# VectorE sums weight and difference for the last twelve weight batches, attention weights loaded in 256 KB transfers, new hand-written orders

## What is computed

```python
x = x + _layernorm(_L0_attn_ref(_layernorm(x), W_qkv, W_out))
x = x + _layernorm(_L0_ffn_ref(_layernorm(x), w_gate_up, w_proj))
# attention: qkv = x @ W_qkv.T ; q, k = phi(q), phi(k)
#   out = q * cumsum(k*v) / (q * cumsum(k) + eps), then @ W_out.T
# feed-forward: weights pass through a per-group ternary quantization
w_g = w.astype(bfloat16).reshape(-1, 64)
scale = clip(mean(abs(w_g)), 1e-8)
w_hat = clip(round(w_g / scale), -1, 1) * scale
wq = w + stop_gradient(w_hat - w)          # all in bfloat16
h = silu(x @ gate) * (x @ up); out = rms_norm(h) @ wq_proj.T
```

## Time and profile before

| what | value |
|---|---|
| median of three runs | 1160.17 us |
| profiled execution, its own time | 1160.26 us |
| its span, first to last instruction | 1158.4 us |
| mean granted TensorE clock | 0.984 of full |
| TensorE matmul busy | 1098.9 us (95%), 5376 matmuls |
| VectorE busy | 772.9 us (67%) |
| ScalarE, GpSimd busy | 442.3 us, 534.2 us |

### The profile page before, as it was taken

One profiled execution on the slowest core, in us unless ns is written; L12 is line 12 of the kernel. 1 busy time (PEld: TensorE's weight loads), 2 busy tenths in 40 slices (PEclk: granted clock), 3 DMA queues, 4 the chain that ended last, 5 costly groups with the idle time before them and its releaser, 6 DMA issues. The chain is left out here.

```text
span 1158.4 us, 14626 instructions
## 1 busy us (share of the span) xinstructions
PE 1098.9 (95%) x5376; PEld 659.5 (57%) x5376; DVE 772.9 (67%) x1224; ACT 442.3 (38%) x752; POOL 534.2 (46%) x493
## 2 busy tenths in 40 slices
PE   6997779998999999999999999999999999899997
PEld 5886355554566864468544774458644684454443
DVE  5999988985668687438872588527863488435323
ACT  3443546665522133422443234431444134333432
POOL 2548789977344343415434254415334253224323
PEclk9998889999999999999999999999999999899999
DMA  7021234200030210002100210002100010100001
GB/s 253 29 73 37 79 88 143 74 29 1 1 109 1 73 37 1 1 1 73 37 1 1 74 37 1 1 1 73 37 1 1 16 58 1 37 1 1 37 1 37
DMA packets 29079, 44.98 MB, mean 39 GB/s; under 512 B 1360, under 2 KB 9552, under 8 KB 29008
## 3 DMA queue, kind: packets, MB, share of 16 engines
q1 hardware_dynamic: 29008, 44.05, 11.7%
HBM read 34.60 MB, written 9.44 MB: 38 GB/s over the span
## 5 line engine op out<-in xcount | busy, mean ns | idle before, releaser
L540 PE MATMUL bank<-x3t,wgu_t 128*128 128x512 f16 x1536 | 351.1, 382 | 11.2 <-ACT ht L946 9.0
L540 PEld LDWEIGHTS bank<-x3t,wgu_t 128*128 128x128 bf16 x1536 | 149.1, 99 | 194.8 <-ACT ht L946 13.9
L1235 POOL TENSOR_TENSOR acc<-acc,ht 128x512 f32<-128x512 f32 x90 | 114.6, 1274 | 270.5 <-ACT ht L987 270.3
L576 PE MATMUL bank<-wproj_t,hid 128*128 128x512 bf16 x872 | 204.8, 380 | 3.3 <-ACT wproj_t L866 3.3
L1594 DVE TENSOR_TENSOR ht<-ht,bank 128x512 f32<-128x512 f32 x112 | 76.1, 679 | 159.8 <-PE bank L540 127.3
L521 PE MATMUL bank<-xnt,wqkv_hi 128*128 128x512 f32 x672 | 168.1, 392 | 0.0
L576 PEld LDWEIGHTS bank<-wproj_t,hid 128*128 128x128 f16 x872 | 85.2, 98 | 104.3 <-issue 4.5
L521 PEld LDWEIGHTS bank<-xnt,wqkv_hi 128*128 128x128 f32 x672 | 125.1, 188 | 26.0 <-issue 0.4
L1600 DVE TENSOR_TENSOR hid<-ht,hid 128x512 f16<-128x512 f32 x109 | 90.6, 831 | 66.3 <-ACT hid L974 66.3
L974 ACT ACTIVATE hid<-ht 128x512 f16<-128x512 f32 x109 | 68.5, 629 | 160.7 <-DVE ht L1594 160.7
L1181 POOL TENSOR_TENSOR tk<-tq,ts 128x512 f32<-128x512 f32 x28 | 55.0, 1965 | 136.6 <-DVE ts L1509 112.7
(11 more groups left out here) (178 smaller groups left out, 1558.2 us busy)
## 6 DMA issues: line engine op xcount, KB each, us to landing
raw_q<-in_L_ffn_w_gate_up_dram SPq DMA_DIRECT2D x32, 256.0 KB, 2.8
xn<-in_L_attn_x_dram SPq DMA_DIRECT2D x7, 1024.0 KB, 5.1
out_dram<-xn SPq DMA_DIRECT2D x7, 1024.0 KB, 8.8
x<-in_L_attn_x_dram SPq DMA_DIRECT2D x6, 1024.0 KB, 6.6
raw_q<-in_L_ffn_w_proj_dram SPq DMA_DIRECT2D x16, 256.0 KB, 2.9
raw_a<-in_L_attn_W_qkv_dram SPq DMA_DIRECT2D x4, 768.0 KB, 8.1
xn<-in_L_attn_x_dram SPq DMA_DIRECT2D x4, 256.0 KB, 3.2
raw_out<-in_L_attn_W_out_dram SPq DMA_DIRECT2D x1, 1024.0 KB, 9.7
```

The source lines that it names most:

```text
L540: last = pe.matmul(bank[:], wgu_t[:, k, first_row:first_row + P], x[:, part, k], start=(n == 0), stop=(n == 2 * KD - 1))
L576: last = pe.matmul(bank[:], hid_of(f, part, k)[:, t * P:(t + 1) * P], wproj_t[:, k], start=(k == 0 and part == 0), stop=(k == MT - 1 and p ...
L1235: pool.tensor_tensor(acc[:], acc[:], ht_of(f)[:, m % 2], ALU.add).then_inc(q["acc_done"], 1)
```

## The change

- **Sum on VectorE.** For batches 12 to 23, a new VectorE call `whole(b)` follows `diff(b)`: yq plus wb into yq, in bfloat16, 128 x 1024. `transpose_half` then waits for `q_whole` and transposes yq alone: 4 matmuls for a half in place of 8. Batches 0 to 11 stay as they are.
- **Attention weights in 256 KB transfers.** Sixteen transfers with a semaphore each in place of five; nine ahead of the wait on the first transposes and seven behind it, as many bytes on each side as before. `transpose_raw(r)` waits for its own tile.
- **Two waits on ScalarE.** `hidden_square` of m == 0 waits for the hidden value alone (`h_done`) in every chunk, no longer for the low part; `hidden_gate` of m == 2 now waits for that low part in every chunk.
- **Orders.** The four lists of `start()` are set anew: the same calls, apart from the twelve `whole`.

```diff
-        raw_a_in = [sem(f"raw_a_in{i}") for i in range(KD + 1)]
+        raw_a_in = [sem(f"raw_a_in{r}") for r in range(4 * KD)]
+        SUMMED = 12
+        q_whole = sem("q_whole")
@@ SyncE
-            def load_raw(i):
-
-                if i < KD:
-                    rows = w_qkv.rearrange("(s j p) k -> p j s k", s=3, p=P)[:, i]
+            def load_raw(r):
+
+                if r < NG:
+                    j, part = divmod(r, 3)
+                    rows = w_qkv[part * D + j * P:part * D + (j + 1) * P, :]
                 else:
-                    rows = w_out.rearrange("(t p) k -> p t k", p=P)
-                sp.dma_start(raw_a[i][:], rows).then_inc(raw_a_in[i], 16)
+                    j, part = KD, r - NG
+                    rows = w_out[part * P:(part + 1) * P, :]
+                sp.dma_start(raw_a[j][:, part], rows).then_inc(raw_a_in[r], 16)
...
-            load_raw(0)
-            load_raw(1)
-            load_raw(2)
+            for r in range(0, 9):
+                load_raw(r)
             sp.wait_ge(t1_done, KD)
             sp.dma_start(xn[:], x_ch[1]).then_inc(x_loaded, 16)
-            load_raw(3)
-            load_raw(4)
+            for r in range(9, 16):
+                load_raw(r)
@@ TensorE
-                    if i == 0:
+                    if i == 0 and b < SUMMED:
                         pe.wait_ge(q_diff, b + 1)
+                    elif i == 0:
+                        pe.wait_ge(q_whole, b - SUMMED + 1)
...
-                        for part, w in enumerate(PLACES[b]):
-                            last = pe.matmul(ps[3][:, n * P:(n + 1) * P], w[:, cols], turned, start=(part == 0), stop=(part == 1))
+                        parts = PLACES[b] if b < SUMMED else PLACES[b][1:]
+                        for part, w in enumerate(parts):
+                            last = pe.matmul(ps[3][:, n * P:(n + 1) * P], w[:, cols], turned,
+                                             start=(part == 0), stop=(part == len(parts) - 1))
...
-                transpose_raw(0, 1), transpose_x_at(0, 0, 1, 2, 3), transpose_raw(2, 3, 4, 5), group_at(0, 0), transpose_raw(6, 7, 8)
+                transpose_raw(0, 1, 2), transpose_x_at(0, 0, 1, 2, 3), transpose_raw(3, 4, 5, 6), group_at(0, 0), transpose_raw(7)
...
-                group_at(1, 0, 1, 2, 3, 4, 5, 6), project_att_at(0, 0, 1, 2, 3), group_at(1, 7, 8, 9, 10), transpose_half(0, 0, 1)
+                transpose_raw(12, 13, 14, 15), group_at(0, 8), transpose_x_at(1, 0, 1, 2, 3), group_at(0, 9, 10, 11), group_at(1, 0, 1, 2, 3, 4)
+                project_att_at(0, 0, 1, 2, 3), group_at(1, 5, 6, 7, 8, 9, 10), transpose_half(0, 0, 1), transpose_x1_at(0, 0, 1, 2, 3)
...
-                transpose_half(22, 0), gate_unit(0, 15), transpose_half(22, 1), project_first(12), up_unit(0, 15), project_first(13)
+                gate_unit(1, 9), gate_unit(0, 15), transpose_half(22, 1), project_first(12, 13), up_unit(1, 9), up_unit(1, 10)
@@ ScalarE
                 elif m == 2:
                     act.wait_ge(q["sq_done"], at(MT, c, 0))
-                    if f < 2:
-                        act.wait_ge(q["h_lo"], 1)
+                    act.wait_ge(q["h_lo"], at(MT, c, 0))
...
-                if f < 2 and m == 0:
-                    act.wait_ge(q["h_done"], 1)
+                if m == 0:
+                    act.wait_ge(q["h_done"], at(MT, c, 0))
                 else:
                     act.wait_ge(q["h_lo"], at(MT, c, m))
...
-                put_half(22, 0), hidden_square(2, 6), hidden_square(1, 13), hidden_hi(1, 14), hidden_gate(2, 8), hidden_square(2, 7)
-                hidden_hi(2, 8), put_half(22, 1), hidden_gate(1, 15), put_half(23, 0), hidden_square(1, 14), hidden_square(2, 8)
+                hidden_square(2, 7), put_half(22, 0), hidden_square(1, 13), hidden_hi(1, 14), hidden_hi(2, 8), put_half(22, 1)
@@ GpSimd
-                scale_back(0), rstd_bias("2", 0), power_take(0), finish_x1_tile(0, 0, 1, 2, 3), scale_back(1), rstd_power("3", 0)
-                rstd_bias("3", 0), norm_x1_tile(0, 0, 1, 2, 3), divide(2), power_lead(1), power_rest(1), power_take(1)
+                power_take(0), scale_back(1, 2), finish_x1_tile(0, 0, 1, 2, 3), den_product(1, 1), divide(3), den_guard(1, 1)
+                power_lead(1), num_product(1, 1), rstd_power("3", 0), divide(4), rstd_bias("3", 0), norm_x1_tile(0, 0)
+                power_rest(1), power_take(1), norm_x1_tile(0, 1, 2, 3), scale_back(3, 4), den_product(1, 2), den_guard(1, 2)
@@ VectorE
+            def whole(*batches):
+
+                for b in batches:
+                    wb, yq = PLACES[b]
+                    dve.wait_ge(q_diff, b + 1)
+                    dve.tensor_tensor(yq[:], yq[:], wb[:], ALU.add).then_inc(q_whole, 1)
...
+                front_products(0, 3), back_reciprocal(0, 2), scale_sums(0), back_output(0, 2), sum_values(0, 3), scale_max(0)
+                back_lo(0, 2), scale_rec(0), back_reciprocal(0, 3), carry_key(0, 3), carry_value(0, 3), back_output(0, 3)
+                feature_k(1, 0), clip(0), back_lo(0, 3), feature_q(1, 0), front_products(1, 0), sum_keys(1, 0), feature_q(1, 1)
+                scale_sums(1), carry_key(1, 0), feature_k(1, 1), stats_tile("2", 0, 0), sum_values(1, 0), sum_keys(1, 1)
+                carry_value(1, 0), scale_max(1), scale_rec(1), scale_row(0), scale_row(1), carry_key(1, 1), stats_tile("2", 0, 1)
+                scale_bound(0), scale_sums(2), scale_max(2), scale_rec(2), stats_tile("2", 0, 2, 3), stats_join("2", 0, 0, 1, 2, 3)
+                stats_mean("2", 0), clip(1), round_off(0), stats_var("2", 0), clip(2), back_reciprocal(1, 0), back_output(1, 0)
+                round_off(1, 2), front_products(1, 1), add_ln2_tile(0, 0), scale_sums(3, 4), diff(0), add_ln2_tile(0, 1), diff(1)
+                add_ln2_tile(0, 2), sum_values(1, 1), add_ln2_tile(0, 3), back_lo(1, 0), carry_value(1, 1), row_shrink(0)
+                stats_tile("3", 0, 0, 1), scale_max(3), scale_rec(3), stats_tile("3", 0, 2, 3), stats_join("3", 0, 0, 1, 2, 3)
+                scale_row(2), scale_row(3), feature_q(1, 2), scale_bound(1), scale_max(4), scale_rec(4), stats_mean("3", 0)
+                stats_var("3", 0), back_reciprocal(1, 1), feature_k(1, 2), back_output(1, 1), sum_keys(1, 2), clip(3, 4)
+                front_products(1, 2), back_lo(1, 1), row_shrink(1), scale_sums(5), carry_key(1, 2), sum_values(1, 2), diff(2)
+                feature_q(1, 3), round_off(3, 4), x3_lo_of(0, 0, 1), scale_max(5), x3_lo_of(0, 2), carry_value(1, 2), scale_rec(5)
+                scale_sums(6), scale_max(6), feature_k(1, 3), x3_lo_of(0, 3), front_products(1, 3), sum_keys(1, 3), sum_values(1, 3)
+                back_reciprocal(1, 2), diff(3), hidden_value(0, 0), carry_key(1, 3), carry_value(1, 3), scale_row(4), scale_row(5)
+                scale_rec(6), scale_bound(2), back_reciprocal(1, 3), back_output(1, 2), back_output(1, 3), clip(5), back_lo(1, 2)
+                back_lo(1, 3), clip(6), round_off(5, 6), scale_sums(7), scale_max(7), scale_rec(7), diff(4), scale_sums(8)
+                hidden_lo(0, 0), scale_max(8), hidden_value(0, 1), scale_rec(8), scale_sums(9), hidden_value(0, 2), scale_row(6)
+                stats_tile("2", 1, 0), scale_max(9), scale_row(7), scale_bound(3), hidden_lo(0, 1), hidden_lo(0, 2), scale_rec(9)
+                clip(7), row_shrink(2), clip(8), stats_tile("2", 1, 1, 2), diff(5), stats_tile("2", 1, 3), stats_join("2", 1, 0, 1)
+                round_off(7, 8), stats_join("2", 1, 2, 3), stats_mean("2", 1), scale_sums(10), stats_var("2", 1), diff(6)
+                scale_max(10), scale_sums(11), add_ln2_tile(1, 0, 1), scale_rec(10), hidden_value(0, 3), add_ln2_tile(1, 2, 3)
+                diff(7), row_shrink(3), clip(9), stats_tile("3", 1, 0), round_off(9), stats_tile("3", 1, 1), clip(10)
+                stats_tile("3", 1, 2, 3), stats_join("3", 1, 0, 1, 2, 3), stats_mean("3", 1), stats_var("3", 1), diff(8)
+                hidden_value(0, 4), hidden_lo(0, 3), round_off(10), scale_sums(12), scale_max(11), scale_rec(11), scale_row(8)
+                scale_max(12), scale_sums(13), scale_rec(12), scale_max(13), hidden_lo(0, 4), scale_rec(13), scale_row(9), diff(9)
+                hidden_value(0, 5), scale_sums(14), x3_lo_of(1, 0, 1), scale_bound(4), diff(10), clip(11), x3_lo_of(1, 2, 3)
+                round_off(11), hidden_lo(0, 5), hidden_value(0, 6), clip(12), scale_sums(15), scale_max(14), scale_rec(14)
...
+                round_off(19), hidden_lo(1, 3), stats_join("1", 2, 0, 1), whole(18), hidden_lo(1, 4), hidden_value(0, 11), diff(19)
```

More of the change, by code:

```diff
@@ L1068, in start @@
[L1068 to L1072 removed]
+                split_weight(0, 1), split_x(0, 0, 1, 2, 3), split_weight(2, 3, 4, 5, 6, 7), feature_relu(0, 0, 0)
@@ L1715, in start @@
-                scale_max(3), front_products(1, 2), scale_row(3), scale_rec(3), scale_bound(1), scale_sums(4), clip(2)
```

(3 more changed lines are left out.)

256 lines of the change are left out of this document (114 added, 142 removed).

## The result

The changed kernel takes 1149.46 us (median of 6 runs, 1147.72 to 1150.55) against 1159.88 us for the kernel before on the same chips (6 runs, 1158.69 to 1161.37): ratio 0.9909, 95% interval 0.9896 to 0.9922. The prediction was 1149.6 us, range 1142 to 1157. The profiled execution took 1149.0 us, its span is 1147.1 us, 11.3 less than before.

What follows compares the result with a forecast made beforehand. TensorE's own work and its stops were taken to make the time (busy 95%). From 1160.3 us, -5.4 - 4.0 - 0.5 + 2.5 - 3.3 = -10.7 gave 1149.6 us, range 1142 to 1157.

Steps and rivals of the forecast that it cites:

- d: Twelve VectorE sums at 0.8 us, 9.6 in all: short VectorE rest makes TensorE wait, tightest near 240 us; +2.5 us.
- c: Opening up to chunk 0's projections: five steps of earlier and later results nearly cancel; -0.5 us, bounds -6 and +4.6.
- a: Half transposes of batches 12 to 23: 96 matmuls go, 0.056 us each, all on the path; -5.4 us.
- b: Stop ahead of project_first(12): only about 1.0 us of 3.30 left, and its lower clock goes; -4.0 us.
- The transfers: Step of c: first weight tile lands sooner, but x transposes wait for GpSimd's norm; at most -0.4 us, later loads nothing.
- TensorE's stop: Step of c: first stop moves from the diff to the norm, some 9 us long; batch 1 starts 6 us later.
- x3_lo(1, 3): Last result of c's stage: 4.6 us more work ahead, most of VectorE's 4.5 us rest recovered; again 180 to 181 us.
- e: Square of hidden tile 0, steps 3 to 7: VectorE's 0.67 us wait for the gate goes in each; -3.3 us.
- Rival 1: The orders give nothing back: waits replace b and add to d, leaving a and e; 1154 to 1158 us, chance 0.20.
- rival 2: The opening gains: VectorE's lead carries through, c is -6 and d near 0; 1139 to 1145 us, chance 0.12.
- Rival 3: Slower: VectorE bounds 100 to 240 us, sums meeting GpSimd's reads take 1.74 us each; 1162.6 us, chance 0.06.
- Rival 4: ScalarE's square held by something else, or VectorE's scans set the pace: 3.3 us less gained, 1153; no own chance.

Runs made afterwards that it cites:

- Experiment 4: The changed kernel, orders kept, without the twelve sums (all halves transposed with 8 matmuls): 1154.27 us, ratio 0.9952.
- experiment 3: The kernel before with only ScalarE's put_half(22, 1) moved ahead of hidden_gate(2, 8), hidden_square(2, 7) and hidden_hi(2, 8): 1154.99 us, ratio 0.9962.
- experiment 1: The changed kernel with ScalarE's two waits put back as they were: 1152.95 us, ratio 0.9942.
- experiment 8: The changed kernel with up_unit(1, 5) ahead of transpose_half(18, 0) and transpose_half(22, 1) ahead of gate_unit(0, 15) in TensorE's list: 1148.35 us, ratio 0.9896.
- experiment 7: The changed kernel with the five large weight transfers of before: 1148.52 us, ratio 0.9900.
- experiment 11: Two runs with the five large transfers of before: on experiment 9, 1150.56 us (ratio 0.9931); on experiment 8, 1146.13 us (ratio 0.9876).
- experiment 10: The changed kernel with back_lo(1, 0) moved ahead of scale_sums(3, 4) in VectorE's list: 1150.23 us, ratio 0.9916.
- experiment 2: The kernel before with ScalarE's two new waits alone: 1156.09 us, ratio 0.9961.
- experiment 9: The kernel of experiment 8 with two more sums, for batches 10 and 11: 1152.39 us, ratio 0.9939.
- experiment 5: The kernel before with the twelve sums alone, each right behind its diff, and halves of 4 matmuls: 1166.81 us, ratio 1.0059.

## Why the prediction held, point by point

The total came out within 0.2 us. Term d did so for another reason than given, and the misses of c and of a term that the sum did not have cancel.

- **a**, the matmuls: -5.4. Experiment 4 measured 5.6 us in the traces, in equal steps. Right.
- **b**, the late stop: -4.0, and 4.0 measured by experiment 3, stop and clock together; in the changed kernel 1.1 us is left, 1.0 was forecast. Right.
- **c**, the opening: -0.5; +0.8 measured, inside its bounds. One pair of traces does not settle its sign: up to here the old lists with large transfers ran in four profiles, and half (10, 0) came at 188.0 to 190.2 us in them, against 189.5 to 190.1 in four with the new lists and small transfers (the changed kernel, experiments 1, 4 and 8). Its steps:
  - *The transfers*: first tile at 7.65, worth nothing in the end, as forecast (ratio 1.0001). That the large ones may be the better choice with the new list (experiments 7 and 11) was not forecast.
  - *back_lo(0, 3)* was forecast for 72.5; the projection started at 70.94 with a wait of about 1 us.
  - *diff(0)* ended at 93.65, 9.3 us earlier in place of 7, its wait is gone.
  - *The norm* ended at 113.2 (near 112 forecast), x3_lo(0, 3) at 120.9 (121.5), batch 1 went to TensorE 5.8 us later (6).
  - *TensorE's stop* was forecast as one of 9 us on the norm and came in pieces: 3.9 at group(1, 10) on ScalarE's tq, 0.7 on a copy, and 5.2 on xn in four waits, the longest 3.3. The first piece is a wait for back_lo(1, 0), which ScalarE's feature map needs:

```profile
98.09 0.60 ACT L910 ACTIVATE tr<-bank 128x512 f32<-128x512 f32 x1 [7.57 <-DVE outt_b L1566]
```

  - The step left out that the new list puts back_lo(1, 0) behind the diffs; experiment 10 shows that this cost nothing there.
  - *The projection of chunk 1* started 3.3 us sooner (4 forecast).
  - *x3_lo(1, 3)* ended at 182.8, 1.8 us past the 180 to 181 of the forecast, and project_first(0) some 2 us past its 181; batch 9's two halves, done ahead, take 0.9 of it back, so that 0.8 us of loss is left when batch 10 begins. The sub-step mis-sized is this one: the list's extra work ahead of x3_lo(1, 3) was paid in greater part than the rest of VectorE could take up.
- **d**, the sums: +2.5. The stops came, 2.3 us in all, and near where it was said: 233, 235 and 241.7. **This is the step that failed in its reason.** Experiment 4 shows the same stops without the sums. The sums themselves were mis-sized too, at 0.8 us each:

```profile
L1407 DVE TENSOR_TENSOR yq<-yq,wb x12: 679/1660/2267, 194.7 to 280.5; 128x1024 bf16<-128x1024 bf16 x12
```

 They take 17.0 us in all, not 9.6, and still cost TensorE next to nothing (one wait of 0.3 us), since the new lists have the diffs done 2.5 to 10.7 us ahead of their transposes, batch 22's 0.8 aside. The median of diff, 0.71 us, was the wrong row; its maximum was the nearer. Beside a large instruction of GpSimd a sum is long, without one short:

```profile
235.16 0.69 DVE L1407 TENSOR_TENSOR yq<-yq,wb 128x1024 bf16<-128x1024 bf16 x1
...
237.20 2.28 POOL L1118 TENSOR_TENSOR yq<-yq,gsc 128x1024 bf16<-128x1024 bf16 x1 [1.30 <-DVE yq L1393]
...
237.79 2.23 DVE L1407 TENSOR_TENSOR yq<-yq,wb 128x1024 bf16<-128x1024 bf16 x1
```

 In the changed kernel seven of the twelve sums are long (1.65 to 2.27 us). A large GpSimd tensor_tensor (1.3 to 2.3 us) was running when each of them began, and each ended 0.54 to 0.55 us after that one did; beside the five short ones (0.68 to 0.69 us) ran small GpSimd instructions of 0.7 us at most, or none. By the Trainium skill, "SBUF — State Buffer", section "Who interferes with whom", a VectorE instruction with two SBUF inputs contends with a GpSimd instruction that reads SBUF, and one waits for the other. The trace agrees: up to 1.6 us a sum, and only the lead hid it.
- **e**, the square: -3.3; 3.7 measured in steps 3 to 7. The mechanism was right; the second stop gives back 0.6 to 0.7 of the 1.3 to 1.5 us, so that 0.75 a step stays and not 0.67. Waits on silu: 6.1 us, five of them, as forecast.
- Not in the sum: 1.1 us behind step 7's stop. It is there in experiments 1 and 2 alike, with the old waits and with the new, and in experiment 7 as a loss of 1.3 us between two kernels with the same steps, so it does not belong to any part of the change. It goes with how long the lower clock lasts after that rest of 4.4 us, 6.8 us in the trace of the kernel before and 3.4 in that of the changed one. The two windows, before and changed:

```profile
985.00:1005.00 20.00, 15.59 (x60) 8.35 (x59) 10.09 (x10) 6.91 (x12) 4.35 (x4) 0.83 0.16 54
```

```profile
985.00:1005.00 20.00, 19.08 (x79) 11.63 (x81) 4.77 (x7) 6.45 (x10) 2.94 (x4) 0.91 0.18 54
```

 In the fourteen profiles six have the 3.4 us there (the changed kernel, experiments 1, 2, 8 and 9, and the first of experiment 11) and gain 0.8 to 1.2 us there on the kernel before; the other eight have 6.8 us, and none gains more than 0.4. Kernels with the changed list of start() and with the old one are found in the first group and in the second, so this term is none of the change's. What decides it is open.

-5.4 - 4.0 + 0.8 + 2.3 - 3.7 - 1.1 = -11.1 of the 11.3 us between the spans. That the total was met to 0.2 us is partly luck: c and the last term differ from the forecast by 1.3 and 1.1 us with opposite signs, and for both of them, traces of variants with the same code up to there differ by about as much.

**The rivals.** Rival 1 (the orders give nothing back) and rival 2 (the opening gains) are out by b and c. Rival 3 had a true mechanism in the wrong place: VectorE does become the bound by the sums where the old lists are kept (7.2 us slower), and where two more sums are added its late results hold TensorE by way of ScalarE (experiment 9). Its chance of 0.06 was for the whole change; the term d had an upper bound of 10.4 us that the old lists pass with 12.6. Rival 4 is out by experiments 1 and 2.

## What to carry to other kernels

Work moved to an engine that is nearly full cost here what its results lost of their lead on the consumer, not its duration: the same twelve adds cost 12.6 us under one order and next to nothing under another. So list each result's lead before and after, and not only that of the moved work: in experiment 9 the results queued behind it did the harm. Reorder in the same change. A stop of the bounding engine is worth its length only if no later wait ends at a fixed time; when it does, removing the stop gives nothing (3.9 us here). A short late stop can be worth nearly twice its length through the clock: 2.1 us of wait, 4.0 of time.

## What was not expected of the hardware

- TensorE's transposes at the start took 0.21 us each, start to start, and from one moment on 0.11 us; that moment came between 13.3 and 18.3 us in the fourteen profiles, and landing the weights 1.8 us sooner did not bring it forward. The granted clock of a window reads 1.00 there only because the record has no entry yet: at the start of a kernel go by the durations.
- After the same rest of 4.4 us in step 7 the lower clock lasted 3.4 us in six profiles and 6.8 us in eight, which moves the total by about 1 us, whatever the change ahead of it.
- The 128x1024 bf16 add with two inputs ran from 0.68 to 2.27 us (median 1.66) in the changed kernel and had a median of 1.96 us in experiment 5, where eight of the twelve met a large GpSimd instruction in place of seven, and six of them took over 2.25 us in place of one.
